# A sandwich of RWKV time mixing and a two-expert MoE on one core: first choices in blocks of their own, one result row per token

## The reference

```python
x = x + layernorm(attn(layernorm(x)))
x = x + layernorm(ffn(layernorm(x)))

# attn: k, v, r from products with Wk, Wv, Wr of x mixed with the token before;
# a running weighted mean over the tokens (wkv, in log space), times sigmoid(r), times Wo

# ffn, per token, E = 8 experts, 2 chosen:
probs = softmax(xf @ router_w);  topw, topi = top_k(probs, 2)
h = silu(xf @ w1[e]);  ye = h @ w2[e]                 # for each chosen expert e
routed = sum over the two choices of topw * ye
gate, up = split(xf @ shared_gate_up)
shared = sigmoid(xf @ shared_gate_w) * ((silu(gate) * up) @ shared_down)
ffn = routed + shared
```

## Time and profile before

| | us |
|---|---|
| median of 3 runs | 1822.88 (1819.39 to 1824.19) |
| the profiled execution, by its own time | 1824.77 |
| span of the profiled execution | 1822.6 |
| busy: PE / DVE / ACT / POOL | 1518.0 / 1466.1 / 1395.4 / 1076.9 |
| moved by DMA | 274.67 MB, 151 GB/s over the span |

### The profile page before, as it was taken

One profiled execution on the slowest core, in us unless ns is written; L12 is line 12 of the kernel. 1 busy time (PEld: TensorE's weight loads), 2 busy tenths in 40 slices (PEclk: granted clock), 3 DMA queues, 4 the chain that ended last, 5 costly groups with the idle time before them and its releaser, 6 DMA issues.

```text
span 1822.6 us, 34848 instructions
## 1 busy us (share of the span) xinstructions
PE 1518.0 (83%) x9764; PEld 1346.6 (74%) x9764; DVE 1466.1 (80%) x3533; ACT 1395.4 (77%) x2577; POOL 1076.9 (59%) x985
## 2 busy tenths in 40 slices
PE   4899999999999999999999935999999999980000
PEld 3688888888888888888888835999888888870000
DVE  4799989999998998989999844887777776764888
ACT  3799999999999999999999853776666666652434
POOL 1245546455563654646555351788888888886556
PEclk8999999999999999999999966999999999995555
DMA  6123434343333433334333234998888888877997
GB/s 202 47 84 118 136 115 139 118 144 105 118 119 106 142 106 107 126 99 142 106 116 108 75 128 158 249 181 144 144 145 146 143 146 143 146 114 232 417 417 299
DMA packets 184043, 274.67 MB, mean 151 GB/s; under 512 B 17712, under 2 KB 139568, under 8 KB 183856
## 3 DMA queue, kind: packets, MB, share of 16 engines
q1 hardware_dynamic: 132688, 201.37, 32.8%
q0 software_dynamic: 51168, 71.07, 22.4%
HBM read 127.53 MB, written 144.85 MB: 149 GB/s over the span
## 4 chain that ended last, share of the span: by engine, by line
PE 51%; issue 12%; POOL 10%; DVE 9%; DMA 9%; ACT 2%; DVEq 2%; SPq 1%; POOLq 0%; ACTq 0%
PE PS L1283 39%; POOL d_y L547 7%; PE PS L1275 3%; PE PS L1459 2%; PE PS L1477 2%; POOL d_xd L522 2%; DMA d_y<-nx,ixb 2%; DMA d_y<-x,ixb 2%; PE PS L1346 2%; PE PS L1344 2%; DMA d_y<-xin,ixb 2%; DVE bst L877 1%; DMA rkl<-d_y 1%; DMA al<-d_y 1%; DMA shl<-d_y 1%
## 5 line engine op out<-in xcount | busy, mean ns | idle before, releaser
L522 POOL DMA_INDIRECT d_xd<-h2n,ixs x256 | 319.4, 1248 | 271.6 <-DVE h2n L1056 190.3
L1283 PE MATMUL PS<-hTh,wqh 128*128 128x512 f32 x768 | 307.4, 400 | 16.8 <-ACT kk L581 11.5
L1283 PE MATMUL PS<-hTh,wql 128*128 128x512 f32 x768 | 306.9, 400 | 0.0
L1283 PE MATMUL PS<-hTl,wqh 128*128 128x512 f32 x768 | 306.5, 399 | 0.0
L1283 PEld LDWEIGHTS PS<-hTh,wqh 128*128 128x128 f32 x768 | 146.8, 191 | 53.0 <-ACT kk L581 12.4
L547 POOL DMA_INDIRECT d_y<-xin,ixb x90 | 143.4, 1593 | 52.5 <-DVE xin L1229 28.5
L1283 PEld LDWEIGHTS PS<-hTh,wql 128*128 128x128 f32 x768 | 146.3, 191 | 34.6
L1283 PEld LDWEIGHTS PS<-hTl,wqh 128*128 128x128 f32 x768 | 146.9, 191 | 33.3
L547 POOL DMA_INDIRECT d_y<-nx,ixb x90 | 142.5, 1584 | 27.4 <-issue 21.9
L547 POOL DMA_INDIRECT d_y<-x,ixb x90 | 142.2, 1580 | 27.4 <-issue 19.8
L482 POOL TENSOR_SCALAR var<-mv 128x4 f32<-128x4 f32 x64 | 64.4, 1006 | 154.4 <-DVE mv L882 154.2
(11 more groups left out here) (301 smaller groups left out, 5631.8 us busy)
## 6 DMA issues: line engine op xcount, KB each, us to landing
d_y<-ysh SPq DMA_DIRECT2D x64, 512.0 KB
xin<-in_L_attn_x SPq DMA_DIRECT2D x32, 512.0 KB, 3.9
x<-in_L_attn_x SPq DMA_DIRECT2D x32, 512.0 KB, 3.9
d_x<-x SPq DMA_DIRECT2D x32, 512.0 KB
kk<-d_xd SPq DMA_DIRECT2D x34, 272.0 KB
vv<-d_xd SPq DMA_DIRECT2D x34, 272.0 KB
tr<-d_xd SPq DMA_DIRECT2D x34, 272.0 KB
dl<-d_xd SPq DMA_DIRECT2D x33, 272.0 KB
```

What stands on the lines that cost most here:

```text
L522: g.indirect_dma_start(d_xd, bass.IndirectOffsetOnAxis(ap=ixs[:, k:k + 1], axis=0), h2n[:, j, :], None).then_inc(s_sct, 16)
L1283: ins = mm_(out_ap, l, r, start=(k == 0), stop=(k == len(todo) - 1))
```

## The change

There are now two tables `d_xd`, one for first and one for second choices, each with its own region per expert, and a third, `d_xs`, for the shared expert's result in the order of the first choices. `d_y` has one row per token.

- Chunk stage: masks, ranks and counts are kept for the two choices apart. SP no longer stores `ysh`; POOL scatters it into `d_xs` with four indirect transfers per chunk (`shared_scatter`). ACT may write `ysh` again when these have landed. The products of TensorE stand in a slightly other order and use other PSUM banks; ACT's `own_exp` stands a step earlier.
- The splitting of the expert weights leaves the steps 17 to 33 and stands in the last steps (34 and 35), when no new chunk comes in.
- Between the stages there are 8 empty blocks for each table. Those of the first `d_xd` are written by SP, those of `d_xs` by ACT after its last chunk, those of the second `d_xd` by SP between the first block loads.
- Block stage: NB1 = 71 blocks for the first choices and 71 for the second, 142 in all. For a first-choice block SP also loads the shared rows into `yb`; DVE multiplies and adds onto them; POOL writes the rows with plain indirect transfers. The second 71 accumulate as before, after all plain ones have landed. The wait in `block_in` is gone.
- Last stage: one `y` piece per chunk, no `total`; ACT writes to another buffer than it reads; 14 `x1` pieces are loaded early.

```diff
-    NB = 2 * N // BLK + E - 1
-    NBP = NB + 1
-    NF = 2 * N // BLK
+    NF = N // BLK
+    NB1 = NF + E - 1
+    NB = 2 * NB1
+    NBP = NB1 + 1
...
-        NS, NY, AHEAD = 12, 6, 4
+        NS, NY, AHEAD = 14, 6, 4
...
@@ sync
             def tails():
 
                 sp.wait_ge(s_zt, 2)
...
+            def tail_2(e):
+                r = sp.value_load(tail[0:1, 1, e:e + 1], min_val=0, max_val=E * CAP - BLK)
+                sp.dma_start(d_xd[1][bass.ds(r, BLK), :].rearrange("(p j) d -> p j d", p=P), zt).then_inc(s_tail2, 16)
...
-                if on(i - 6):
-                    sp.wait_ge(s_ys, n(i - 6, NT, NT))
-                    for s in range(2):
-                        sp.dma_start(ys_a[s, i - 6], ysh[:, :, :]).then_inc(s_st2, 16)
...
             sp.wait_ge(s_sct, 16 * 2 * NT * NCH)
-            sp.wait_ge(s_tail, 16 * (E + 1))
+            sp.wait_ge(s_tail, 16 * (2 * E + 3))
+            sp.wait_ge(s_scy, 16 * NT * NCH)
...
+            def load_shared(b):
+                if b >= NYB:
+                    sp.wait_ge(s_yo[b % NYB], 32 * (b // NYB))
+                r = sp.value_load(tabx[0:1, 0, b:b + 1], min_val=0, max_val=E * CAP)
+                sp.dma_start(yb[b % NYB], d_xs[bass.ds(r, BLK), :].rearrange("(p j) d -> p j d", p=P)
+                             ).then_inc(s_yl[b % NYB], 16)
...
             for b in range(NB):
+                if b == NB1:
+                    sp.wait_ge(s_tail2, 16 * E)
                 load_block(b)
+                if 1 <= b <= E:
+                    tail_2(b - 1)
+                if b == 8 + 10:
+                    sp.wait_ge(s_tail2, 16 * E)
+                if 0 <= b - 2 < NB1:
+                    load_shared(b - 2)
                 if b >= 8 and b - 8 < NS:
                     load_rest(b - 8)
...
-                    sp.dma_start(y0C[c % NY], y_v[0, c]).then_inc(s_cy2[c % NY], 16)
-                    sp.dma_start(y1C[c % NY], y_v[1, c]).then_inc(s_cy2[c % NY], 16)
+                    sp.dma_start(yC[c % NY], y_v[c]).then_inc(s_yl[c % NY], 16)
@@ gpsimd
+            def shared_scatter(m):
+                pool.wait_ge(s_pl, n(m, NPL, L_IX))
+                for j in range(NT):
+                    pool.wait_ge(s_ys, n(m, NT, j + 1))
+                    g.indirect_dma_start(d_xs, bass.IndirectOffsetOnAxis(ap=ixs[:, m % 2, j:j + 1], axis=0),
+                                         ysh[:, j, :], None).then_inc(s_scy, 16)
...
+                if w < NB1:
+                    for j in range(2):
+                        g.indirect_dma_start(d_y, bass.IndirectOffsetOnAxis(ap=ixb[:, w % 8, j:j + 1], axis=0),
+                                             yb[w % NYB][:, j, :], None).then_inc(s_yo[w % NYB], 16)
+                else:
+                    if w == NB1:
+
+                        for i in range(NYB):
+                            pool.wait_ge(s_yo[i], 32 * ((NB1 - i + NYB - 1) // NYB))
@@ scalar
                 act.wait_ge(s_wt, n(m, NWT, W_SG))
                 if m:
-                    act.wait_ge(s_st2, 32 * m)
+                    act.wait_ge(s_scy, 16 * NT * m)
...
+            act.wait_ge(s_zt, 2)
+            act.wait_ge(s_tab, 1)
+            for e in range(E):
+                r = act.value_load(tail[0:1, 0, e:e + 1], min_val=0, max_val=E * CAP - BLK)
+                A.dma_start(d_xs[bass.ds(r, BLK), :].rearrange("(p j) d -> p j d", p=P), zt[:, :, 0:D]).then_inc(s_tail, 16)
@@ vector
+                    if w < NB1:
+                        V.scalar_tensor_tensor(out=t, in0=part, scalar=cwb[:, w % 8, j:j + 1], in1=t, op0=ALU.mult,
+                                               op1=ALU.add).then_inc(s_y, 1)
+                    else:
+                        V.tensor_scalar(t, part, cwb[:, w % 8, j:j + 1], None, ALU.mult).then_inc(s_y, 1)
...
-            def total(c):
-                dve.wait_ge(s_cy2[c % NY], 32 * (c // NY + 1))
-                if c >= NO:
-                    dve.wait_ge(s_out[c % NO], 16 * (c // NO))
-                V.tensor_tensor(oC[c % NO], y0C[c % NY], y1C[c % NY], ALU.add).then_inc(s_sum, 1)
-                dve.wait_ge(s_sum, c + 1)
@@ tensor
                 for a in range(H):
-                    if a and t >= 4:
-                        pe.wait_ge(s_yp, t - 3)
                     for j in range(2):
```

More of the change, by code:

```diff
@@ L52, in rwkv_moe @@
     out_c = out.rearrange("b (c p j) d -> (b c) p (j d)", j=NT, p=P)
-    d_xd = nc.dram_tensor("d_xd", [E * CAP + BLK, XW], F32).ap()
-    NSINK = E + NB - NF + 1
-    d_y = nc.dram_tensor("d_y", [2 * N + 1 + NSINK * BLK, D], F32).ap()
-    ys_a = d_y[1:2 * N + 1, :].rearrange("(s c j p) d -> s c p j d", s=2, j=NT, p=P)
+    d_xd = [nc.dram_tensor(f"d_xd{s}", [E * CAP + BLK, XW], F32).ap() for s in range(2)]
+    d_xs = nc.dram_tensor("d_xs", [E * CAP + BLK, D], F32).ap()
+    NSINK = E + NB1 - NF + 1
+    d_y = nc.dram_tensor("d_y", [N + 1 + NSINK * BLK, D], F32).ap()
     with ExitStack() as ctx:
@@ L275, in rwkv_moe @@
         s_yo = [sem(f"s_yo{i}") for i in range(6)]
+        s_yl = [sem(f"s_yl{i}") for i in range(6)]
         s_Tx = sem("s_Tx")
@@ L286, in rwkv_moe @@
         s_y = sem("s_y")
-        s_cx = [sem(f"s_cx{i}") for i in range(12)]
-        s_cy2 = [sem(f"s_cy2{i}") for i in range(6)]
-        s_sum = sem("s_sum")
+        s_cx = [sem(f"s_cx{i}") for i in range(14)]
         s_nrm = sem("s_nrm")
@@ L297, in rwkv_moe @@
         NRO = 7
-        L_POS, L_TB, L_PM, L_POSA, L_IX, L_MT, L_DST = range(1, 8)
-        NPL = 7
+        L_POS, L_TB, L_PM, L_POSA, L_IX, L_DST = range(1, 7)
+        NPL = 6
         W_SUM, W_CWT, W_SG, W_CW = range(2, 6)
@@ L314, in rwkv_moe @@
         hidB, outB = PS[2:5], PS[5:8]
-        zt = xb[1]
+        zt = ee[:, :, :].rearrange("p a t -> p (a t)")[:, 0:2 * XW].rearrange("p (j d) -> p j d", j=2)
         yb = [t[:, i:i + 2, :] for i in (0, 2) for t in (xin, nx, x1)]
         NYB = len(yb)
+        NYL = [(NB1 - i + NYB - 1) // NYB for i in range(NYB)]
+        assert NYB == 6
         xTh = [hTh[:, 0, 0:TC], rkh[:, 0, :]]
@@ L386, in _ @@
             sp.dma_start(x1[:, :, :], x_v[0]).then_inc(s_xr, 16)
-            for i in range(NCH + 6):
+            for i in range(NCH + 4):
                 if i % 2 == 0 and i // 2 < E:
@@ L475, in _ @@
             for e in range(E):
[L476 removed]
+                last = g.memset(tb[:, :, e:e + 1], float(e * CAP))
             last.then_inc(s_const, 1)
@@ L545, in _ @@
                 pool.wait_ge(s_y, 2 * (w + 1))
-                for j in range(2):
-                    g.indirect_dma_start(d_y, bass.IndirectOffsetOnAxis(ap=ixb[:, w % 8, j:j + 1], axis=0),
-                                         yb[w % NYB][:, j, :], None, compute_op=ALU.add).then_inc(s_yo[w % NYB], 16)
+                if w < NB1:
[6 more added lines that the diff above has]
+                            pool.wait_ge(s_yo[i], 32 * ((NB1 - i + NYB - 1) // NYB))
+                    for j in range(2):
+                        g.indirect_dma_start(d_y, bass.IndirectOffsetOnAxis(ap=ixb[:, w % 8, j:j + 1], axis=0),
+                                             yb[w % NYB][:, j, :], None, compute_op=ALU.add).then_inc(s_yo[w % NYB], 16)
             for c in range(NCH):
@@ L1187, in _ @@
             step(4)
[L1188 to L1192 removed]
+            for s in range(2):
+                V.tensor_tensor_scan(cum[:, s, :], ones8[:, :], nbk[:, s, :], zero[:, 0:1], ALU.mult, ALU.add).then_inc(s_tb, 1)
@@ L1202, in _ @@
             step(11)
+            both = [P, 2, NBP]
+            V.tensor_tensor(tbf[:, 1, :, :], tbf[:, 1, :, :], iot2[:, :].unsqueeze(1).to_broadcast(both), ALU.add
+                            ).then_inc(s_tb, 1)
+            step(12)
             V.tensor_scalar(iot2[:, :], iot2[:, :], -(NF - 1.0) * BLK, None, ALU.add).then_inc(s_tb, 1)
-            step(12)
-            V.scalar_tensor_tensor(out=tabo[:, :], in0=tbf[:, 0, :], scalar=E - 0.5, in1=iot2[:, :], op0=ALU.is_ge,
-                                   op1=ALU.mult).then_inc(s_tab, 1)
```

253 lines of the change are left out of this document (134 added, 119 removed).

## The result

The changed kernel takes 1791.21 us (median of 4 runs, 1790.16 to 1793.26) against 1822.88: ratio 0.983, 95% interval 0.981 to 0.985. The forecast was 1800, range 1780 to 1828. Its profiled execution took 1793.26 us.

What follows compares the result with a forecast made beforehand. TensorE was full in the chunk stage, POOL the limit in the block stage, DMA full in the last. Terms -41.4 + 3 - 7.5 + 7.2 + 15.2 = -23.5 us gave a forecast of 1800 us, range 1780 to 1828.

Steps and rivals of the forecast that it cites:

- Last stage: Last stage: one `y` piece instead of two and 14 early `x1` pieces instead of 12 give -41 us.
- Rival C: Last stage: stays near 4.4 us per chunk by the loop DVE, POOL, ACT, DVE; -13 us, 1828; chance 0.07.
- Block stage: 142 blocks: first 71 at TensorE's 3.40 us, last 71 at POOL's 3.78, 2.3 us between; +3 us.
- Rival A: Block stage: first 71 blocks stay at 3.78 us because plain scatters cost POOL the same; +27, 1827; chance 0.10.
- The wait for own products: Block stage: TensorE's wait is mostly hidden by two transposes, so removing it gives 0, at most -23 us.
- Steady steps: Chunk stage: the expert copies leave the steady chunks; -7.5 us, bounds -8.5 and 0.
- Drain: End of chunk stage: expert copies now delay the last chunks; +7.2 us, bounds 0 and 8.3.
- End of the stage: Chunk stage's end: shared scatters, ACT's activations and tail writes, then SP's load delay the first block; +15.2 us.
- POOL in the steady steps: Chunk stage: POOL's four added scatters per chunk fit in its gaps; 0 us.
- Rival E: Chunk stage: POOL's added work does not fit and chunks lengthen; +36 us, 1836; chance 0.05.
- B: Block stage: shared rows load late, deciding from a 12.9 us load on; +57 us, 1857; chance 0.08.
- Rival D: Chunk stage's end overlaps better and the own-product wait is worth a few us; 15 us less, 1785; chance 0.13.

Runs made afterwards that it cites:

- e8: Changed kernel whose last stage loads each chunk's row of results a second time into a buffer nobody reads; 1855.9 us (one run), last stage 155.2 us.
- e7: Changed kernel with SP's eight tail writes of second choices issued before the block stage; 1830.5 us, 1.005 to the kernel before.
- e11: Changed kernel with the edits of e5 and e7, and the last chunk's scaled rows put in `nx`; 1824.2 us, 1.001 to the kernel before.
- e2: Kernel before with only PE's wait for its own products taken away; 1824.0 us, ratio 0.9996.
- e3: Changed kernel with the splitting of the experts' weights back in steady steps 17 to 33; 1825.6 us, 1.001 to the kernel before.
- e10: Changed kernel with PE's second half of the up product back behind the first half of the key product; 1828.2 us, 1.003 to the kernel before.
- e5: Changed kernel with ACT's eight tail writes of `d_xs` issued ahead of its last scaled rows; 1823.0 us, 1.001 to the kernel before.

## Why the prediction was right, point by point

**Last stage: right** (-42.6 for -41.4), mechanism shown by e8. A chunk with `x1` loads was put at 3.77 us and takes 3.75. One without them was put at 3.15 and takes 2.91 where nothing but DVE holds it, so the stage came out a little shorter than forecast. Rival C (4.4 per chunk) is out.

**Block stage: right in sum** (+3.3 for +3), with parts that cancel. The second half was put at 268.4 and took 268.1. The first half was put at 241.4 plus 2.3 and took 245.2. It runs at 3.34 per block, not 3.40 (-4.3 us over 71); against that stand the slow first twelve blocks (+3.4), where SP issues three DMAs per block (e7 and e11 point to that as the cause and do not show it), single later blocks that take a little longer than 3.34 (+1.1, what remains), and the change of halves: POOL starts to add 3.6 us after its last plain scatter has ended, of which 2.3 were counted (+1.3). That these come to +1.5, and the stage to within 0.3 us, is luck. Rival A is out: 1.14 us against 1.57 for the same 128 rows, a mean of 1.12 over all plain ones against the 1.248 taken from the chunk stage.

The mean of the plain scatters lies 0.17 us over the shortest, 0.96, and the trace shows what lengthens them. POOL and DVE in the changed kernel, one scatter of a block:

```profile
1240.67 1.29 POOL L578 DMA_INDIRECT d_y<-xin,ixb  x1 [0.30 <-issue]
1241.04 0.87 DVE L1293 SCALAR_TENSOR_TENSOR nx<-PS,cwb,nx 128x256 f32<-128x256 f32 x2
```

The scatter ends 0.05 us after DVE's multiply-add. So it is with 54 of the 59 plain scatters that take over 1.1 us. The 67 that run in part beside a multiply-add take 1.25 us in the mean, the 75 others 1.01, though nearly all of these run beside DVE's cast, copy or differences. The rule that the prediction weighed (the Trainium skill, "SBUF — State Buffer", section "SBUF: two separate sides") speaks of a copy in a two-port mode, and would have the mean 0.48 us over the shortest if every scatter met one. Here DVE's cast and copy hardly lengthen a scatter (no row shows in which mode they ran), and the new multiply-add does. Since PE is the limit in this half, it costs no time.

**The wait for own products: put at 0, worth some 4 us**, because PE really is the limit in the first half. The argument that two transposes hide the first 0.3 us of it was wrong by 0.06 us per block, and 71 of these count (4.3 us, an estimate from the two paces; no run measures the sum). That it gives nothing where POOL is the limit is shown by e2.

**Steady steps: -7.5 forecast.** In the 15 steps -8.9 came. The copies cost 7.8 to 10.3 there by e3 and the kernels with the same condition; 15 x 0.08 = 1.2 of the 8.9 is the step itself, which fell from 31.91 to 31.83, so 7.7 is left for the copies. The 0.08 per step had been bounded at +-0.1 and put at 0; over the 28 steps up to 988 it is 2 us, and e10 points to the order of the products. With it and an earlier start, the time up to the second mark fell by 10.8 us for the 7.5 forecast.

**Drain: +7.2 forecast for the copies, 9.5 measured by e3.** But the drain as a whole, up to the first scatter of the last chunk, grew by only 5.9 (109.9 to 115.7 us). The other edits must give 3.6 us there; no run says which. The term for the copies was 2.3 us too small, and the term for the rest, put at nothing, hid it.

**End of the stage: +15.2 forecast, +12.5 measured** (22.0 to 34.5 us from POOL's first scatter of the last chunk to the first block). The chain is the predicted one, and e5 shows its last link, 4.5 us. Mis-sized by 2.7 us: activations and tail writes were laid end to end, 11.9 us, and took some 10.5 (1122.25 to 1132.70 in the chain), since the first write is already issued at 1123.34, beside the activations; SP's last step and the load were put at 4.4 us and took 3.8 from the landing at 1135.10. The remaining 0.7 lie mostly before: from the first scatter of the last chunk to ACT's first activation 18.6 us were put and 17.8 taken.

**POOL in the steady steps: 0, right.** It is busier by 128 scatters of 1.05 us, and the steps stayed at 31.83. Rival E is out, and so is B: DVE's multiply-add in the first half does not hold PE up, which is busy 40 of 40 us in the stretch shown, and the shared rows land 3.1 to 3.4 us (median by buffer) after their issue, where B begins at 12.9.

**Rival D** (1785 us) lies 6.2 us from the result, the forecast 8.8. Of its parts the own-product wait came true. The copies were not hidden, and the tails took 1.4 us less than forecast, not 5; what brought the time towards it are the steady steps and the edits in the drain that no term has.

Summed up: the forecast was 8.8 us high. The start of the block stage makes 6.7 of it (3.3 up to the end of the steady steps, 1.3 in the drain, 2.7 at its end, less 0.6 from the first block to its scatter) and the last stage 1.2; the block stage was 0.3 longer than forecast; the rest, 1.2, is rounding and the time around the span.

## What to carry to other kernels

Cut bytes where the stretch shows DMA full, and count only the bytes: a load that nobody used cost 31 of the 43 us that its removal together with its sum had given. An edit that makes one engine's step shorter is worth what the next limit leaves: the same wait was worth nothing with POOL at 3.78 us per block and 0.06 us per block once PE was the limit. Moving work out of a full stage into its drain was a swap of 8 to 10 us for 9.5 us: look at who waits in the drain before calling it free.
